# Turning feed-forward inputs and outputs in 32x32 blocks on VectorE and through DRAM, with GpSimd adding the residual

## The reference, cut to what matters

```
x = layernorm(x + attention(x))            # 16 heads of 8, ALiBi bias, softmax
h = silu(x @ w1.T * s1) * (x @ w2.T * s2)  # 128 -> 512
h = gelu(h @ h1.T * t1)                    # 512 -> 512
h = gelu(h @ h2.T * t2)                    # 512 -> 512
y = h @ w3.T * s3                          # 512 -> 128
out = layernorm(x + y)
```

## Time and profile before

| | |
|---|---|
| time, median of 3 runs | 802.08 us (801.79 to 804.29) |
| profiled execution | 799.74 us, its span 797.9 us |
| TensorE busy | 769.2 us, 96% of the span |
| VectorE | 630.1 us, 79% |
| ScalarE | 611.7 us, 77% |
| GpSimd | 313.4 us, 39%, nearly all of it in the first 446 us |
| DMA | 102 GB/s on average; 39 GB/s or so in the feed-forward part |
| granted TensorE clock | 0.9 or more of full speed in every fortieth of the span but the last (0.8) |

### The profile page before, as it was taken

How to read it: one execution, slowest core, us unless ns; L and a number is a source line. 1 busy time by engine, 2 the same in 40 slices (tenths; PEclk the granted TensorE clock), 3 DMA queues, 4 the chain that set the end, 5 groups by cost and what they waited for, 6 DMA issues and landing times.

```text
span 797.9 us, 26869 instructions
## 1 busy us (share of the span) xinstructions
PE 769.2 (96%) x10370; PEld 557.4 (70%) x10370; DVE 630.1 (79%) x1303; ACT 611.7 (77%) x1096; POOL 313.4 (39%) x490
## 2 busy tenths in 40 slices
PE   4999999999999999999999999999999999999995
PEld 2566666666666666666665788888888888888873
DVE  4789899899989999989993767777777776666774
ACT  5588787888888888878878777777777777777762
POOL 5346878787756657575634200000000000000001
PEclk9999999999999999999999999999999999999998
DMA  6755565656556565564621100111111111101001
GB/s 181 190 145 166 168 185 159 195 151 182 164 159 166 141 181 136 170 174 144 174 65 44 41 27 28 39 41 39 39 39 39 31 34 39 39 26 40 16 26 54
DMA packets 107341, 81.37 MB, mean 102 GB/s; under 512 B 11168, under 2 KB 94112, under 8 KB 107232
## 3 DMA queue, kind: packets, MB, share of 16 engines
q1 hardware_dynamic: 105632, 76.59, 34.1%
q0 software_dynamic: 880, 2.88, 1.3%
q10 hardware_dynamic: 720, 0.36, 0.2%
HBM read 45.72 MB, written 33.55 MB: 99 GB/s over the span
## 4 chain that ended last, share of the span: by engine, by line
PE 92%; DVE 2%; DMA 2%; issue 2%; ACT 1%; POOL 1%; SPq 0%; POOLq 0%; ACTq 0%; DVEq 0%
PE ps_b L951 17%; PE ps_b L954 17%; PE ps_o L523 15%; PE ps_a L464 11%; PE ps_b L472 6%; PE ps_b L579 4%; PE ps_a L951 3%; PE ps_a L954 3%; PE ps_a L548 2%; PE ps_a L479 2%; PE ps_b L540 2%; PE ps_a L562 2%; PE ps_b L479 2%; PE ps_b L570 1%; PE ps_b L534 1%
## 5 line engine op out<-in xcount | busy, mean ns | idle before, releaser
L762 DVE TENSOR_REDUCE neg_sb<-ps_a 128x2 f32<-128x512 f32 x512 | 324.7, 681 | 37.1 <-PE ps_a L479 29.7
L654 ACT ACTIVATE probs<-ps_b 128x512 f32<-128x512 f32 x512 | 281.4, 591 | 57.2 <-PE ps_b L479 57.1
L464 PE MATMUL ps_a<-qk_stack 52*64 52x256 bf16 x2048 | 178.0, 281 | 5.6 <-DMA qk_stack<-qk_scratch 2.8
L472 PE MATMUL ps_b<-qk_stack 54*64 54x256 bf16 x2048 | 172.3, 276 | 1.1 <-ACT probs L654 0.9
L1062 ACT ACTIVATE gelu_f<-ps_b,sc 128x512 f32<-128x512 f32 x124 | 85.5, 690 | 74.0 <-PE ps_b L954 66.4
L464 PEld LDWEIGHTS ps_a<-qk_stack 52*64 52x64 bf16 x2048 | 82.5, 108 | 79.4 <-DVE neg_sb L762 61.0
L523 PE MATMUL ps_o<-probs,v_aug 128*32 128x256 f32 x2048 | 137.3, 385 | 0.0
L1224 POOL TENSOR_SCALAR vareps_f<-meanvar_f 128x4 f32<-128x4 f32 x15 | 9.7, 644 | 301.0 <-DVE meanvar_f L1125 301.0
L479 PE MATMUL ps_a<-corner_sb,eye_sb 64*64 64x128 bf16 x1024 | 116.4, 222 | 0.3 <-issue 0.3
L479 PE MATMUL ps_b<-corner_sb,eye_sb 64*64 64x128 bf16 x1024 | 114.4, 218 | 0.0
L951 PE MATMUL ps_b<-g2h,h_hi 128*128 128x512 f32 x256 | 102.7, 401 | 0.0
(11 more groups left out here) (124 smaller groups left out, 1429.3 us busy)
## 6 DMA issues: line engine op xcount, KB each, us to landing
qk_stack<-qk_scratch SPq DMA_DIRECT2D x128, 192.0 KB, 3.4
qk_scratch<-qk_sb SPq DMA_DIRECT2D x64, 192.0 KB, 3.0
qk_scratch<-qk_sb SPq DMA_DIRECT2D x96, 128.0 KB, 3.0
xT_sb<-in_xT SPq DMA_DIRECT2D x32, 128.0 KB, 3.5
x_sb<-in_x SPq DMA_DIRECT2D x32, 128.0 KB, 3.4
x_scratch<-x_sb SPq DMA_DIRECT2D x32, 128.0 KB, 3.4
x_in<-x_scratch SPq DMA_DIRECT2D x32, 128.0 KB, 2.1
x_res<-x_scratch SPq DMA_DIRECT2D x32, 128.0 KB, 2.1
```

The costliest lines, as they stand in the source:

```text
L464: pe.matmul(ps[side * TILE:(side + 1) * TILE, qb * SEQ:(qb + 1) * SEQ], q_stack[i][rows_of, j, at:at + TILE], k_stack[i][rows_of, j, :], s ...
L472: pe.matmul(ps[side * TILE:(side + 1) * TILE, kb * SEQ:(kb + 1) * SEQ], k_stack[i][rows_of, j, at:at + TILE], q_stack[i][rows_of, j, :], s ...
L654: nc.scalar.activation(probs[:, h % HALF, :], ps_b[b_bank(t, k)][:], ACT.Exp, scale=slope[h]).then_inc(exp_done, 1)
L762: nc.vector.tensor_reduce(negmax[:, h_a // HALF, h_a % GROUPS, h_a % HALF // GROUPS, :], ps_a[a_bank(t, k)][:].rearrange("p (b k) -> p b k ...
```

## The change

TensorE's turns of the inputs of chunks 3 to 15 and of the outputs of chunks 0 to 13 are taken out (13 and 14 groups of four). In their place VectorE transposes 32x32 blocks within a 128x512 tile, and DMAs regroup the blocks.

- **Input.** `load_blocks` reads x1 from DRAM with four DMAs, one for each 32 features, so that on partition g*32+i stands row i of each of the 16 row blocks, 32 features (128 B) at a time. One VectorE transpose then gives `xT_f` in SBUF, and GpSimd makes `xh` (copy) and `xl` (subtraction) from it.
- **Output.** VectorE transposes `y_sb` into `y_turn`; four DMAs write it to `y_scratch` in runs of 128 B; when they have landed, one DMA reads `y_rows` back with rows on partitions, and GpSimd adds `x_res` to it. This add stands one step later than before.
- **Order.** On VectorE `stats` moves from the end of the step to between g2l and the gates, and `normalise(c-2)` from before the gates to behind g1l. On SyncE the four block stores, the wait for them, a wait for the previous residual add and the load of `y_rows` are appended to the step.
- **Layout.** `x1_scratch` becomes [8192, 128]; `load_chunk` is one DMA of 256 KB in runs of 512 B, and the store of x1 has runs of 512 B too.

```diff
-def load_chunk(sp, x1_dram, c, dst, signal):
+def load_chunk(sp, dram, c, dst, signal):
+    sp.dma_start(dst[:], dram.rearrange("(c a p) d -> c p a d", a=CB, p=P)[c]).then_inc(signal, DMA)
...
+        TURNED_FROM = 3
+        LAST_TURNED = CHUNKS - 3
+        def turned_by_pe(c):
+            return isinstance(c, int) and c < TURNED_FROM
+        def y_by_blocks(c):
+            return not isinstance(c, int) or 0 <= c <= LAST_TURNED
+        x_blocks, y_blocks = (dram.rearrange("(c j i) (g f) -> c g i j f", j=CHUNK // SQUARE, i=SQUARE, f=SQUARE)
+                              for dram in (x1_dram, y_dram))
+        def load_blocks(sp, c):
+            for g in range(P // SQUARE):
+                sp.dma_start(x_in[g * SQUARE:(g + 1) * SQUARE, :, :].rearrange("p a d -> p (a d)").rearrange(
+                    "p (j f) -> p j f", f=SQUARE), x_blocks[c, g]).then_inc(xblk_landed, DMA)
@@ SyncE @@
                     wait_apart(sp, xT_done, c + 3, passed["sp"])
-                    load_chunk(sp, x1_dram, c + 3, x_in, xin_landed)
+                    if isinstance(c, int) and c + 3 < TURNED_FROM:
+                        load_chunk(sp, x1_dram, c + 3, x_in, xin_landed)
+                    else:
+                        load_blocks(sp, c + 3)
...
+                if y_by_blocks(c - 1):
+                    wait_apart(sp, y_turned, c, passed["sp"])
+                    for g in range(QUADS):
+                        sp.dma_start(y_blocks[c - 1, g], y_turn[g * SQUARE:(g + 1) * SQUARE, :].rearrange(
+                            "p (j f) -> p j f", f=SQUARE)).then_inc(y_written, DMA)
+                    wait_apart(sp, y_written, c * QUADS * DMA, passed["sp"])
+                    wait_apart(sp, res_done, c - 1, passed["sp"])
+                    load_chunk(sp, y_dram, c - 1, y_rows, y_landed)
@@ TensorE @@
-                if live(c + 2, CHUNKS) and not (isinstance(c, int) and c == 0):
+                if turned_by_pe(c + 2) and c != 0:
                     turn_x(c)
...
-                    else:
+                    elif not y_by_blocks(c - 1):
                         wait(pe, y_copied, c)
@@ VectorE @@
-                if live(c - 2, CHUNKS) and not (isinstance(c, int) and c == CHUNKS):
-                    normalise(c - 2)
+                if y_by_blocks(c - 2):
+                    stats(c - 1)
...
+                if y_by_blocks(c - 2):
+                    normalise(c - 2)
+                if turned_by_pe(c + 2):
                     wait(dve, x_hi, c + 3)
                     nc.vector.tensor_tensor(xl, ps_x[:], xh.bitcast(F32), ALU.subtract).then_inc(x_lo, 1)
+                elif live(c + 2, CHUNKS):
+                    wait_apart(dve, xblk_landed, (c + 3 - TURNED_FROM) * QUADS * DMA, passed["dve"])
+                    wait_apart(dve, x_lo, c + 2, passed["dve"])
+                    nc.vector.transpose(xT_f[:], x_in[:].rearrange("p a d -> p (a d)")).then_inc(xT_done, 1)
...
+                elif y_by_blocks(c - 1):
+                    wait_apart(dve, y_copied, c, passed["dve"])
+                    wait_apart(dve, y_written, (c - 1) * QUADS * DMA, passed["dve"])
+                    nc.vector.transpose(y_turn[:], y_sb[:]).then_inc(y_turned, 1)
...
-                if live(c - 1, CHUNKS) and not last and not (isinstance(c, int) and c == CHUNKS):
-                    stats(c)
@@ GpSimd @@
+                if y_by_blocks(c - 2):
+                    wait_apart(pool, y_landed, (c - 1) * DMA, passed["pool"])
+                    wait_apart(pool, xres_landed, (c - 1) * DMA, passed["pool"])
+                    wait_apart(pool, out_done, c - 2, passed["pool"])
+                    nc.gpsimd.tensor_tensor(res[:].rearrange("p a d -> p (a d)"), y_rows[:].rearrange("p a d -> p (a d)"),
+                                            x_res[:].rearrange("p a d -> p (a d)"), ALU.add).then_inc(res_done, 1)
+                    root(c - 2)
+                if live(c + 2, CHUNKS) and not turned_by_pe(c + 2):
+                    wait_apart(pool, xT_done, c + 3, passed["pool"])
+                    wait_apart(pool, up_in, (c + 2) * KT, passed["pool"])
+                    nc.gpsimd.tensor_copy(xh, xT_f[:]).then_inc(x_hi, 1)
+                    wait_apart(pool, x_hi, c + 3, passed["pool"])
+                    nc.gpsimd.tensor_tensor(xl, xT_f[:], xh.bitcast(F32), ALU.subtract).then_inc(x_lo, 1)
```

More of the change, by code:

```diff
@@ L73 @@
 SPILLS = 5
+SQUARE = 32
 XT_BUFS = 6
@@ L221, in norm_x1, with x1_rows @@
     ins.then_inc(carried.x1_done, 1)
-def load_chunk(sp, x1_dram, c, dst, signal):
-    for n in range(CHUNK // SEQ):
-        sp.dma_start(dst[:, n * BLK:(n + 1) * BLK, :],
-                     x1_dram.rearrange("(c n) p a d -> c p n a d", n=CHUNK // SEQ)[c, :, n, :, :]).then_inc(signal, DMA)
+def load_chunk(sp, dram, c, dst, signal):
+    sp.dma_start(dst[:], dram.rearrange("(c a p) d -> c p a d", a=CB, p=P)[c]).then_inc(signal, DMA)
+def x1_rows(x1_dram, b):
+    return x1_dram.rearrange("(b a p) d -> b p a d", a=BLK, p=P)[b]
 class Tail:
@@ L388, in step @@
                     wait(sp, x1_stored, (t - 3) * DMA)
-                    sp.dma_start(x1_dram[t - 3], x1_sb[1 - par][:]).then_inc(x1_stored, DMA)
+                    sp.dma_start(x1_rows(x1_dram, t - 3), x1_sb[1 - par][:]).then_inc(x1_stored, DMA)
                 if live(t, BATCH):
@@ L590, in step @@
                 if t == BATCH:
-                    pe.wait_ge(carried.xin_landed, CHUNK // SEQ * DMA)
+                    pe.wait_ge(carried.xin_landed, DMA)
                     pe.wait_ge(max_done, BATCH * HEADS)
@@ L867, in attention, with ffn @@
     return tail
-def ffn(nc, block, wts, x1_dram, out, carried, tail):
+def ffn(nc, block, wts, x1_dram, y_dram, out, carried, tail):
     (w1h, w1l), (w2h, w2l), (h1h, h1l), (h2h, h2l), (w3h, w3l) = wts
@@ L895, in ffn @@
         y_out = sb("y_out", [P, CB, D])
+        xT_f = sb("xT_f", [P, CHUNK])
+        y_turn = sb("y_turn", [P, CHUNK])
+        y_rows = sb("y_rows", [P, CB, D])
         ps_r, ps_s, ps_x, ps_y = tail.ps_r, tail.ps_s, tail.ps_x, tail.ps_y
@@ L901, in ffn @@
         xres_landed, out_stored = sem("xres_landed"), sem("out_stored")
+        xblk_landed = sem("xblk_landed")
+        y_written, y_landed = sem("y_written"), sem("y_landed")
         silu_in, up_in, silu_done, gate_done = sem("silu_in"), sem("up_in"), sem("silu_done"), sem("gate_done")
@@ L918, in ffn @@
         NB = CHUNK // SEQ
+        TURNED_FROM = 3
+        QUADS = P // SQUARE
+        LAST_TURNED = CHUNKS - 3
[9 more added lines that the diff above has]
+                    "p (j f) -> p j f", f=SQUARE), x_blocks[c, g]).then_inc(xblk_landed, DMA)
         @block.sync
@@ L931, in step @@
                     wait_apart(sp, xT_done, c + 3, passed["sp"])
-                    load_chunk(sp, x1_dram, c + 3, x_in, xin_landed)
+                    if isinstance(c, int) and c + 3 < TURNED_FROM:
+                        load_chunk(sp, x1_dram, c + 3, x_in, xin_landed)
+                    else:
+                        load_blocks(sp, c + 3)
                 if isinstance(c, int) and c == 0:
                     sp.wait_ge(carried.x1_done, BATCH)
-                    sp.dma_start(x1_dram[BATCH - 1], carried.x1_sb[(BATCH - 1) % 2][:]).then_inc(carried.x1_stored, DMA)
+                    sp.dma_start(x1_rows(x1_dram, BATCH - 1), carried.x1_sb[(BATCH - 1) % 2][:]).then_inc(carried.x1_stored, DMA)
                 if isinstance(c, int) and c == 1:
                     sp.wait_ge(carried.x1_stored, BATCH * DMA)
+                if y_by_blocks(c - 1):
[6 more added lines that the diff above has]
+                    load_chunk(sp, y_dram, c - 1, y_rows, y_landed)
             drive(sp, step, **STEPS)
@@ L964, in turn_x @@
             def turn_x(c):
-                wait(pe, xin_landed, (c + 3) * NB * DMA)
+                wait(pe, xin_landed, (c + 3) * DMA)
                 wait(pe, x_lo, c + 2)
@@ L990, in step @@
                         pe.wait_ge(tail.res_done, BATCH)
-                    wait(pe, res_done, c - 1)
+                    if y_by_blocks(c - 2):
+                        wait(pe, y_copied, c - 1)
+                    else:
+                        wait(pe, res_done, c - 1)
                     product(ps_y, 0, w3h, lows["w3"], g3h, g3l, KT,
@@ L1086, in step @@
                             nc.scalar.activation(g1h[:, i, :], gate_f[:, i, :], ACT.Copy).then_inc(g1_hi, 1)
-                if live(c + 2, CHUNKS):
+                if turned_by_pe(c + 2):
                     wait(act, xT_done, c + 3)
@@ L1131, in finish @@
                 dve.wait_ge(y_turned, c + n + 1)
-                dve.wait_ge(xres_landed, CHUNKS * NB * DMA)
+                dve.wait_ge(xres_landed, CHUNKS * DMA)
                 dve.wait_ge(out_done, c)
@@ L1189, in step @@
                         finish(n)
+                elif y_by_blocks(c - 1):
+                    wait_apart(dve, y_copied, c, passed["dve"])
```

(22 more changed lines are left out.)

## The result

The changed kernel takes 792.78 us (median of 4 runs, 792.41 to 795.68), the kernel before 801.93 beside it (4 runs). The ratio is 0.9902, 95% interval 0.9882 to 0.9921: 9.2 us faster, where I forecast 17 us slower and gave "faster" a third. The profiled execution took 792.41 us, its span is 790.6. Both ran again in a later comparison: 793.13 against 800.35, ratio 0.9898 (0.9869 to 0.9926).

A forecast was written before the change was run, and what follows sets the result against it. TensorE bounded the old kernel; the loop through DRAM would set 23.1 us steps. Terms +19.7, -0.4, -1.1 and -0.9 gave +17.3 us: 819.4 us from the 802.08 median, likeliest range 806 to 839, whole range 789 to 842.

The forecast's parts named there:

- What bounds, and the price of a turn: TensorE bounds at 21.46 us a step; four turns cost 0.435 us, 27 groups 11.7 us, leaving 20.59 us steps.
- VectorE's transposes: Two new fp32 transposes of 128x512 a step, taken at 0.68 us each, at most 2.7; VectorE's load stays 15.3 us.
- The round: Loop from VectorE through DRAM and GpSimd's add back to VectorE's gates and next transpose; 23.1 us taken, against TensorE's 20.59.
- the packet term: In the DRAM trip, y_out's store and both block sets share a queue limited by packet number; y written at N + 9.7.
- N: The end of VectorE's `normalise`, from which the prediction counts the times of the loop through DRAM.
- my other end: In the DRAM trip, y's block stores limited by SyncE's issues instead of packets: y written at N + 7.0.
- The 0.59 per ns: Packet limit for the DMA queue, from 59 tiny scale packets in 100 ns; gives 3.6 us per set of 128 B packets.
- The line between 7.5 and 28 ns: Engine time per DMA packet, interpolated between tiny and 512 B packets: 12.7 ns at 128 B, 1.7 us a set.
- my 20.4 at the low end: Low estimate in us of the loop through DRAM, if issues limit y's stores; just under TensorE's 20.59.
- the slack that is used once: Stats and gates could finish before the h2 product needs them; 1.1 us subtracted once from the forecast sum.
- issue sets the round: Faster rival: 128 B packets at 12.7 ns, loop of 20.4 us, TensorE still bounds, 790.4 us; chance 0.32.
- Doubled packet time for stores to DRAM: Slower rival: 128 B stores to DRAM cost twice, y set 7.2 us, loop 26.7 us, 863 us; chance 0.15.

The follow-up runs named there:

- experiment 2: Changed kernel with SyncE issuing the four block stores of y ahead of the four block loads of x: 789.02 us, ratio 0.9848 to the kernel before.
- experiment 8: Changed kernel with xh and xl made by ScalarE and VectorE instead of GpSimd: 794.83 us, ratio 0.9915 to the kernel before.
- experiment 3: Changed kernel with the block loads of x as eight DMAs of 32 KB instead of four: 813.1 us, ratio 1.0142 to the kernel before.
- experiment 9: Changed kernel with the block loads of x in 64 B runs instead of 128 B, same bytes: 802.8 us, ratio 1.0016 to the kernel before.
- experiment 7: Changed kernel with eight block loads of x, issued behind the load of y_rows: 789.13 us, ratio 0.9832 to the kernel before.
- experiment 4: Changed kernel without y's stores and load; GpSimd adds the unregrouped y_turn: 790.04 us, ratio 0.9864 to the kernel before.

## Why the prediction was wrong, step by step

- *What bounds, and the price of a turn*: right. 0.435 us for four turns gives steps of 21.03 with one side and 20.59 with both; measured 21.03, 21.02 and 20.59. All 27 groups should be worth 11.7 us; experiment 2, where nothing else is late, is 800.35 - 789.02 = 11.3 us faster.
- *VectorE's transposes*: I took 0.68; they take 0.70 and 0.67. Its load didn't stay at 15.3 us a step but rose to 148.2 / 9 = 16.5, mostly by what GpSimd does beside g3l (experiment 8).
- *The round*: its mechanism was right. It exists, it sets the step, and each 0.49 us of issues ahead of y's stores adds to it (experiment 3: +1.94 us of issues, +1.8 a step).
- **The step that failed is the packet term**: "limited by packets ... 0.25 + 1.4 + (544 + 2112 + 2112) / 590 = N + 9.7". Measured, the last store has landed at N + 7.3, close to my other end, N + 7.0. The block stores are 1.9 us from issue to landing, like the 128 KB stores of `y_out` in the kernel before: they don't queue behind the 2112 packets of x. The 0.59 per ns came from one tenth of a microsecond of one 144-packet DMA, which may be over before the full rate is reached, and the changed kernel passes 1.03 to 1.39 per ns. I chose it although the row itself showed engines 72% idle. The line between 7.5 and 28 ns, which I set aside, said 12.7 ns; 12.6 (loads) and 12.9 (stores) are measured.
- *The terms beside it*: issues of a block DMA take 0.49 and not 0.46 (eight of them, 0.2), and the last block store is issued at N + 4.9 instead of 4.6; `y_rows` and its hand-over 3.1 to 3.4 instead of 2.8 and the add 1.29 instead of 1.17; VectorE's part 8.9 instead of 9.2. With N + 7.3 the round comes to 20.9 to 21.4, and with my 20.4 at the low end TensorE would have bound. Nine steps of 21.04 mean that the round still costs 0.45 us a step.
- *The sum redone*: 802.08 - 11.7 + 12 x (21.04 - 20.59) = 795.8, and less up to 1.1 for the slack that is used once: 794.7, two over the 792.8 measured. The two us are no more than what the kernel before moves by: its medians in the comparisons lie between 800.35 and 802.46. From the 800.35 of the later one the same sum gives 793.0, and 793.13 was measured there; the spans, 797.9 and 790.6, differ by 7.3, and the sum has 7.4. The 1.1 of slack isn't measured by itself.
- *The rivals*: the one that came true is "issue sets the round", at a round of 21.04, within its "to 21.3 the result is still faster", and so without TensorE quite binding. Doubled packet time for stores to DRAM: refuted, the stores land in 1.9 us, the loads of the same size in 2.1, at 12.9 and 12.6 ns a packet.
- *Slips beside the sum*: "in PSUM 0.3 us after ScalarE's copy". In the step of the earlier trace rows that copy ends at 565.35 and the turns start at 566.65, behind w2. No term rests on it. The chances of the cases, 0.32 for faster and 0.46 + 0.15 for slower, are a hundredth off the closing 0.33 and 0.60.

The Trainium skill (DMA: Bandwidth & Descriptors, Specifications) says that below 512 B the SDMA does a read-modify-write. No price of it shows here. The packets lie near the prediction's line, a fixed part of some 7.5 ns and 0.04 ns a byte: 10.7 ns at 64 B (experiment 9), 12.6 and 12.9 at 128 B, 28 at 512 B, without a step below 512. A small packet is dearer per byte, 46% of the time for a quarter of the bytes, by that fixed part. Whether a second pass takes place none the less, no run shows.

## What to carry to other kernels

A round trip through DRAM in a software pipeline costs only if the loop that it closes, from one engine's list back to the same place in that list, is longer than the bounding engine's step; add it up link by link, and count every DMA issue ahead of it on the issuing engine, here at half a microsecond. Here what was issued behind the trip was free (experiment 7), and what was issued ahead of it was paid almost in full (1.8 of 1.94 us, experiment 3): order the queue by who waits, not by who is ready first. A rate read from a short burst says what passed and not what could pass: 0.59 and 0.95 packets per ns looked like limits, and 1.39 and 1.75 were read elsewhere.

## What the runs showed of the hardware

- Packets of 128 B: 12.6 ns (loads) and 12.9 ns (stores) of an engine each, 1.39 per ns over all sixteen in the busiest 0.2 us. Packets of 64 B from DRAM: 1.75 per ns over 0.4 us, 116.4% x 400 x 16 / 699 = 10.7 ns each.
- SyncE issues four DMAs of 512 runs in 1.96 us (0.49 each), eight of 256 runs in 3.90 (0.49 each), and four of 1024 runs in 2.62, of which the third and fourth are the long ones (0.65 against 0.36 and 0.42).
- GpSimd slows VectorE. Beside GpSimd's cast and subtraction (571.32 to 573.64) the four g3l subtractions took 3.89 us, and 2.45 in experiment 8, where GpSimd has neither. The Trainium skill (SBUF — State Buffer, Who interferes with whom) says that a VectorE instruction with two SBUF inputs contends with a GpSimd instruction that reads SBUF; by this rule g3l, which reads `gelu_f` and `g3h`, must suffer, and the trace agrees, with 1.44 us a step. In experiment 4 GpSimd's add follows at once on the subtraction, beside g3l too, and the four take 4.98 us (571.08 to 576.06). I had not counted it; it cost nothing, since the steps were no shorter in experiment 8 and stayed at 20.58 us in experiment 4. GpSimd's own subtraction took 1.53 us against 1.27 in the first part; whether VectorE slows it isn't shown.
